# Front projections in two rounded passes, centred key weights turned on the array, and ten of sixteen heads on VectorE

## The chip, the cores and the metric

The kernel runs on one NeuronCore of a Trainium2 chip. The metric is the device time of one execution in microseconds (us); lower is better. A program is written for each engine by hand (TensorE, here PE; VectorE, DVE; ScalarE, ACT; GpSimd, POOL; SyncE, SP, which issues the loads), and the engines meet only at semaphores. Each engine runs its own list in order.

## The reference

A small network with 8 x 32 tokens of width 256 and a context of 8 x 512 tokens. The change touches only the first layer's attention, and in it the projections and the norms of their heads:

```
ln_out = LN(layernorm(x)) * ln_w + ln_b                     # 256 tokens x 256
def lin(x, w, w_scale, in_scale):
    xq = fp8(bf16(clip(x / in_scale, -448, 448)))           # rounded to 4 bits of mantissa
    return (xq * in_scale) @ w.T * w_scale
qx = LN(lin(ln_out, wqx, ...))      # 16 heads of 128
k  = LN(lin(ln_out, wk, ...))       #  8 groups of 128
q  = LN(lin(ln_out, wq, ...))       # 16 heads of 128
v  = lin(ln_out, wv, ...)           #  8 groups of 128
kx, vx = split(ctx @ w_kv_x.T);  kx = LN(kx)
cat = [softmax(q k / sqrt(128)) v, softmax(qx kx / sqrt(128)) vx]
x = x + lin(cat, wproj, ...)
```

A state-space layer, a mixture of experts, attention to the masked context, an attention with rotary positions and a table-coded feed-forward layer follow. They are as they were.

## The kernel before

The front is everything ahead of the loop over the eight batches of context. It has three strands:

- **Projections.** The weights come in six chunks of 1024 columns (`VARIANT` says which of the four input scales a chunk uses: 0 and 1 are the cross queries, 2 the keys, 3 and 4 the queries, 5 the values). `project(n)` makes four banks of 128 tokens x 512 columns, each from two products in fp32 (`CT` is 2), with the rounded inputs `xs` held in the array and the chunk `wch` streamed. An fp32 product stands in the trace as two matmul instructions, so a chunk is 16 of them. The input scale is multiplied into `xs` on DVE (L1735). Chunks use two slots of `wch`; a chunk is loaded when the one two before it has been used.
- **Head norms.** ACT reads the four banks (`read_chunk`, L1612) into one of two slots of `raw`. DVE takes the statistics of 16 heads (`norm_heads`, L1756) and prepares the variance (L1759 to L1763), ACT does Ln and Exp (L283, L284), DVE a Newton step and the shift (L263 to L1770), and then each engine scales 8 heads: DVE at L1775, ACT at L1632 in `normalise`. PE turns the 16 heads (`turn`, L1514), ACT reads them (`read_turn`, L1639).
- **Cross queries.** DVE multiplies the turned heads by a column (`read_turn_cross`, L1786); PE then makes `beta` and eight products `A` for chunk n against the centred key weights `wkc` (`cross_queries`, L1524 and L1529), each into a bank of a ring of four (`RING`) that ACT must have read (L1598, L1621) before it comes round again.

The key weights are centred twice: `wkc` (natural order) by a product with a centring matrix (L1571), and `wkT` (turned) on DVE by a sum, a scaling and a subtraction (L1743 to L1745) from a load of its own. `wk_hi` and `wk_lo` (L1659, L1800) are a rounded fp32r copy of `wkT` and what it leaves, and are needed for `keys` (L429 to L431), the first work of the loop, which already runs in rounded passes; so is `ctx_lo` (L684).

The orders are written out by hand. On PE: centre, project 0, project 1, turn 0, project 2, cross queries 0, turn 1, project 3, cross queries 1, turn 2, project 4, turn 3, project 5, core scores, then keys and turn 4. The orders on ACT and DVE are seen in the diff and in the functions below.

Of the kernel before, what the change touches and what calls it, by code (L numbers as in the profile page):

```python
# [17 lines left out]
T = B * S  # L18
# [29 lines left out]
for _name, _w in [("ident", 128), ("ones", 128), ("center", 128), ("mixed", S), ("cos", S), ("sin", S), ("iota", LUTN)]:  # L48
# [12 lines left out]
    ("ctx_hi0", CT * NK, FRONT, LOOP), ("beta", NH * T, FRONT, LAST), ("A_hi", CT * NK, FRONT, LAST),  # L61
# [5 lines left out]
    ("kT", G * T, FRONT, FRONT), ("v", TT * 1024, FRONT, FRONT), ("attn", 4 * 512, FRONT, FRONT),  # L67
# [33 lines left out]
RING = [("lnT", 4, "dve"), ("center", 4, "act")]  # L101
# [18 lines left out]
def build(nc, io, out):  # L120
    ctx = ExitStack()
    with ctx:
# [12 lines left out]
        for name in ("wkc", "wkT", "ctx_hi0", "ctx_hi1", "ctxT_ring", "A_hi", "A", "catx", "A_first", "beta"):  # L135
            tensors[name, fp32r] = tensor(name, fp32r)
# [71 lines left out]
        ld_const, ld_x, ld_wkn, ld_wkT, ld_wvT = (sem(n) for n in ("ld_const", "ld_x", "ld_wkn", "ld_wkT", "ld_wvT"))  # L208
# [13 lines left out]
        xs_ready, wk_centered, bk_ready = sem("xs_ready"), sem("wk_centered"), sem("bk_ready")  # L222
# [76 lines left out]
        def round_fp8(step, n, dst):  # L299
# [6 lines left out]
            return nc.vector.tensor_tensor(dst, dst, m_bf[:, 0:n], ALU.subtract)  # L306
# [37 lines left out]
        wpx_lo, wpx_hi = buf("A_first", NH, C, dtype=fp32r), buf("beta", NH, C, dtype=fp32r)  # L344
# [1081 lines left out]
        def _(sp):  # L1426
# [5 lines left out]
            sp.dma_start(wkT, io["wkT"]).then_inc(ld_wkT, 16)  # L1432
# [38 lines left out]
        def _(pe):  # L1471
# [19 lines left out]
            def project(n):  # L1491

                pe.wait_ge(xs_ready, SCALED.index(VARIANT[n]) + 1)
                pe.wait_ge(ld_chunk[n % 2], 16 * (n // 2 + 1))
                for q in range(4):
                    j, hf = q // 2, q % 2
                    if n:
                        pe.wait_ge(proj_read, 4 * n - 3 + q)
                    for c in range(CT):
                        last = nc.tensor.matmul(bank(q), xs[:, VARIANT[n], c, j * 128:j * 128 + 128],  # L1500
                                                wch[n % 2][:, c, hf * 512:hf * 512 + 512],
                                                start=c == 0, stop=c == CT - 1)
                    last.then_inc(proj_full, 1)

            def turn(n):
# [3 lines left out]
                for i in range(4):  # L1509
                    o = bank(ring(f"turn{n}", i), 2, T)  # L1510
                    for k in range(4):
# [3 lines left out]
                                                   raw[RAW_SLOT[n]][:, j, c0:c0 + 128], ident)  # L1515
                    last.then_inc(ring_full, 1)
# [56 lines left out]
            project(0)  # L1573
            project(1)
# [15 lines left out]
        def _(act):  # L1590
# [4 lines left out]
            def read_ring(name, i, dst, **kw):  # L1595
# [3 lines left out]
                                     ACT.Copy, **kw).then_inc(ring_read["act"], 1)  # L1599

# [24 lines left out]
            def normalise(n):  # L1625
# [4 lines left out]
                for i in range(8):  # L1630
# [12 lines left out]
            act_rstd(act, step, TT, 1)  # L1643
            for i in range(4):
# [12 lines left out]
            act.wait_ge(ring_full, RING_AT["A1"] + 8)  # L1657
            act.wait_ge(wk_centered, 1)
# [44 lines left out]
        def _(dve):  # L1703
# [21 lines left out]
            def scaled_input(n):  # L1725
# [7 lines left out]
                step(round_fp8(step, CT * T, xs[:, n].rearrange("p c t -> p (c t)")))  # L1733
                for c in range(CT):
                    last = nc.vector.tensor_scalar(xs[:, n, c, :], xs[:, n, c, :], col("in_scale", n * CT + c), None,  # L1735
                                                   ALU.mult)
                last.then_inc(xs_ready, 1)
                dve.wait_ge(xs_ready, SCALED.index(n) + 1)

            scaled_input(0)  # L1740
            dve.wait_ge(ld_wkT, 16)
            heads = wkT.rearrange("p c (g d) -> p (c g) d", g=G)
            step(nc.vector.tensor_reduce(nt[:, 0:CT * G], heads, AX, ALU.add))  # L1743
            step(nc.vector.tensor_scalar(nt[:, 0:CT * G], nt[:, 0:CT * G], 1.0 / D, None, ALU.mult))
            nc.vector.tensor_tensor(heads, heads, nt[:, 0:CT * G].unsqueeze(2).broadcast_to([128, CT * G, D]),  # L1745
                                    ALU.subtract).then_inc(wk_centered, 1)

            def norm_heads(n):
# [24 lines left out]
                for i in range(8):  # L1773
                    hd = r[:, 0, i * D:(i + 1) * D]
# [159 lines left out]
```

## Time and profile before

| | |
|---|---|
| time, median of 3 runs | 479.61 us (478.98 to 480.41) |
| the profiled execution | 483.38 us, of it the span 481.6 us |
| PE busy | 450.2 us (93%) |
| DVE busy | 352.0 us (73%) |
| ACT busy | 248.7 us (52%) |
| mean granted TensorE clock | 0.982 of full speed |

The span runs from the first to the last instruction of the profile. Busy times count an engine's instructions at work, not its waits. Lines (L1500) are those of the kernel before.

### The profile page before, as it was taken

Reading aid. Unit: us, or ns where it says so; the run is one execution under the profiler, and the core shown is the slowest. Engines: PE = TensorE matmul, PEld = TensorE weight load, DVE = VectorE, ACT = ScalarE, POOL = GpSimd, SP = SyncE. Lnnn points to the kernel's source line nnn. Section 1 sums busy time; section 2 is a strip of 40 time slices with the busy share of each in tenths; the row PEclk is TensorE's granted clock in tenths of the full one; section 3 lists DMA queues with packets and bytes.
Section 4 is the critical chain, followed back from the end, with each engine's and each line's share of the span. In section 5 each row is a group of like instructions: output and inputs, shape, how many; then the busy total and the mean of one; then the engine's idle time right before and its main releaser. Section 6 shows DMA issues by size and latency. Waiting matters only on the chain.

```text
span 481.6 us, 6644 instructions
## 1 busy us (share of the span) xinstructions
PE 450.2 (93%) x2336; PEld 304.9 (63%) x2342; DVE 352.0 (73%) x729; ACT 248.7 (52%) x784; POOL 25.5 (5%) x33
## 2 busy tenths in 40 slices
PE   5987999989999999999999999998888999989897
PEld 2442445667887676767576776856655888536566
DVE  5888495849799869698899989766776468644731
ACT  1465688997553677758986676553020205110120
POOL 0000000000110000101001010100000111100000
PEclk9999799999999999999999999999998999989999
DMA  8167020224201114693448464880068579720000
GB/s 314 82 228 297 0 88 0 79 99 160 82 0 45 44 45 109 136 319 70 110 109 172 111 131 110 177 333 0 1 206 329 176 206 222 166 85 1 1 1 22
DMA packets 14046, 58.57 MB, mean 122 GB/s; under 512 B 1792, under 2 KB 2496, under 8 KB 12480
## 3 DMA queue, kind: packets, MB, share of 16 engines
q1 hardware_dynamic: 10992, 41.66, 23.6%
q0 software_dynamic: 3024, 16.52, 17.6%
q8 instruction: 17, 0.28, 0.2%
q14 instruction: 13, 0.11, 0.1%
HBM read 41.40 MB, written 0.26 MB: 87 GB/s over the span
## 4 chain that ended last, share of the span: by engine, by line
PE 74%; DVE 12%; ACT 10%; issue 2%; DMA 1%; SPq 0%; DVEq 0%; ACTq 0%
PE PS L456 11%; PE PS L429 9%; PE PS L431 8%; PE PS L430 8%; PE PS L1043 6%; PE PS L1529 3%; PE PS L1500 3%; PE PS L476 3%; PE PS L1054 3%; ACT raw_dt.float L1632 3%; PE PS L503 2%; PE PS L1154 2%; ACT raw_dt.float L1612 2%; PE PS L465 1%; PE PS L364 1%
## 5 line engine op out<-in xcount | busy, mean ns | idle before, releaser
L576 ACT ACTIVATE sq_dt.float<-PS 128x128 bf16<-128x128 f32 x256 | 67.3, 281 | 28.9 <-PE PS L431 22.2
L456 PE MATMUL PS<-s_dt.float,ctx_ring_dt.float 128*128 128x512 f32 x128 | 57.7, 593 | 1.3 <-DVE px_dt.float L810 1.3
L429 PE MATMUL PS<-wkc_dt.float32r,ctx_hi_dt.float32r 128*128 128x512 f32 x128 | 53.7, 420 | 1.6 <-ACT sq_dt.float L576 1.2
L576 ACT ACTIVATION_READ_ACCUMULATOR sq_dt.float<-PS 128x1 f32 x256 | 53.8, 211 | 0.0
L431 PE MATMUL PS<-wkc_dt.float32r,ctxT_ring_dt.float32r 128*128 128x512 f32 x128 | 50.4, 393 | 0.0
L430 PE MATMUL PS<-wkT_dt.float32r,ctx_hi_dt.float32r 128*128 128x512 f32 x128 | 50.1, 392 | 0.0
L653 ACT ACTIVATE luttmp_dt.float<-low_bit_dt.float,vec_dt.float,small_dt.float 128x1536 f32<-128x1536 uint8 x24 | 38.5, 1656 | 10.5 <-DMA lutw_dt.float<-luttmp_dt.float 10.5
L1500 PE MATMUL PS<-wch_dt.float,xs_dt.float 128*128 128x512 f32 x96 | 42.2, 594 | 0.7 <-DVE xs_dt.float L1735 0.7
L456 PEld LDWEIGHTS PS<-s_dt.float,ctx_ring_dt.float 128*128 128x128 f32 x128 | 23.6, 190 | 25.0 <-issue 23.0
L660 DVE SCALAR_TENSOR_TENSOR luttmp_dt.float<-idx_dt.float,luttmp_dt.float 128x1536 f32<-128x1536 uint8 x21 | 36.5, 1750 | 0.0
L364 PE MATMUL PS<-consts_dt.float 128*128 128x512 bf16 x116 | 28.9, 404 | 6.0 <-DMA consts_dt.float<-in_consts 5.5
L429 PEld LDWEIGHTS PS<-wkc_dt.float32r,ctx_hi_dt.float32r 128*128 128x128 f32 x128 | 24.0, 187 | 14.1 <-ACT sq_dt.float L576 9.3
L1500 PEld LDWEIGHTS PS<-wch_dt.float,xs_dt.float 128*128 128x128 f32 x96 | 17.8, 190 | 22.3 <-issue 20.3
L666 POOL DMA_DIRECT2D lutw_dt.float<-luttmp_dt.float x21 | 18.3, 871 | 188.2 <-DVE luttmp_dt.float L660 188.2
L431 PEld LDWEIGHTS PS<-wkc_dt.float32r,ctxT_ring_dt.float32r 128*128 128x128 f32 x128 | 24.0, 188 | 5.7
L430 PEld LDWEIGHTS PS<-wkT_dt.float32r,ctx_hi_dt.float32r 128*128 128x128 f32 x128 | 24.1, 188 | 3.6
L797 DVE TENSOR_TENSOR s_dt.float<-s_dt.float,PS 128x2048 f32<-128x2048 f32 x8 | 18.3, 2288 | 10.3 <-PE PS L446 10.3
L364 PEld LDWEIGHTS PS<-consts_dt.float 128*128 128x128 bf16 x122 | 12.1, 103 | 21.0 <-DMA consts_dt.float<-in_consts 5.5
L429 PE MATMUL PS<-A_hi_dt.float32r,ctx_hi_dt.float32r 128*128 128x512 f32 x64 | 25.3, 396 | 0.0
L430 PE MATMUL PS<-A_dt.float32r,ctx_hi_dt.float32r 128*128 128x512 f32 (+1 forms) x64 | 24.9, 390 | 0.0
L431 PE MATMUL PS<-A_hi_dt.float32r,ctxT_ring_dt.float32r 128*128 128x512 f32 x64 | 24.9, 389 | 0.0
L283 ACT ACTIVATE small_dt.float<-small_dt.float 128x2 f32<-128x2 f32 (+1 forms) x12 | 3.7, 304 | 37.6 <-DVE small_dt.float L274 30.1
(272 smaller groups left out, 845.0 us busy)
## 6 DMA issues: line engine op xcount, KB each, us to landing
lutw_dt.float<-luttmp_dt.float POOLq DMA_DIRECT2D x21, 768.0 KB, 6.6
wch_dt.float<-in_chunks SPq DMA_DIRECT2D x6, 1024.0 KB, 5.0
ctxT_ring_dt.float<-in_ctxT SPq DMA_DIRECT2D x8, 512.0 KB, 4.0
ctx_ring_dt.float<-in_ctx SPq DMA_DIRECT2D x8, 512.0 KB, 3.3
keysT_dt.float<-in_ctxT SPq DMA_DIRECT2D x8, 512.0 KB, 7.6
keys_dt.float<-in_ctx SPq DMA_DIRECT2D x8, 512.0 KB, 9.3
luttmp_dt.float<-in_idx SPq DMA_DIRECT2D x3, 768.0 KB, 5.6
zu_dt.float<-in_wproj SPq DMA_DIRECT2D x1, 2048.0 KB, 7.3
```

The source lines that it names most:

```text
L364: nc.tensor.matmul(bank(nb), busy[:, 0:128], busy, start=True, stop=True)
L429: nc.tensor.matmul(o, x_hi, hi[:, c, :], start=c == 0, stop=False)
L430: nc.tensor.matmul(o, x_hi, lo[:, c, :], start=False, stop=False)
L431: last = nc.tensor.matmul(o, x_lo, hi[:, c, :], start=False, stop=c == CT - 1)
L456: last = nc.tensor.matmul(bank(5 + c), keysr[k][:, t, c * 128:c * 128 + 128], sS[k][:, t, :], start=t == 0, stop=t == KT - 1)
L576: last = nc.scalar.activation(sq[:, (4 * hf + g) * D:(4 * hf + g + 1) * D], bank(hf)[:, g * D:(g + 1) * D], ACT.Square, accum_out=ssq[:, k ...
L653: nc.scalar.activation(lutt[:, m, :], low_bit[:, m, :], ACT.Identity, scale=lut_gap[:, k:k + 1], bias=col("lut", 2 * k)).then_inc(lut_leaf, 1)
L660: nc.vector.scalar_tensor_tensor(lutt[:, m, :] if k else lutw[:, m, :], idx[:, m, :], float(2 * k), lutt[:, m, :], ALU.is_equal, ALU.mult) ...
L666: pool.dma_start(lutw[:, m, :], lutt[:, m, :], accum_op=ALU.add).then_inc(lut_added[m], 16)
L797: nc.vector.tensor_tensor(sS[k], sS[k], bank(4).unsqueeze(1).broadcast_to([128, KT, 512]), ALU.subtract)\
L1043: last = nc.tensor.matmul(o[:, m, :], wgu[e % 4][:, i, w0:w0 + 128], hT[:, c, :], start=c == 0, stop=c == CT - 1)
L1500: last = nc.tensor.matmul(bank(q), xs[:, VARIANT[n], c, j * 128:j * 128 + 128], wch[n % 2][:, c, hf * 512:hf * 512 + 512], start=c == 0, s ...
```

## The change

1. A chunk of weights is multiplied by its input scale and rounded to fp32r by ACT (`wch_hi`), DVE makes what the rounding leaves (`wch_lo`, in place of the chunk), and `project` runs an fp32r pass for each. `xs` is written in fp32r and no longer scaled (L1735 goes).
2. `wkT` is no longer loaded and centred on DVE. PE turns `wkc` (`turn_wk`, 16 transposes in four banks, between project 0 and project 1) and ACT copies it out.
3. DVE scales 10 of the 16 heads, ACT the other 6.
4. In the order of ACT `normalise(2)` moves from ahead of `read_chunk(3)` to behind `cross_queries(1)`; in that of DVE `read_turn_cross(1)` moves ahead of `norm_heads(2)`. The splits are put between.
5. Buffers: `wch_hi0`, `wch_hi1` and a `wpx_hi` of its own; `beta` gets smaller.

```diff
-RING = [("lnT", 4, "dve"), ("center", 4, "act")]
+RING = [("lnT", 4, "dve"), ("center", 4, "act"), ("wkturn", 4, "act")]
...
-            sp.dma_start(wkT, io["wkT"]).then_inc(ld_wkT, 16)
...
             def project(n):
                 pe.wait_ge(xs_ready, SCALED.index(VARIANT[n]) + 1)
-                pe.wait_ge(ld_chunk[n % 2], 16 * (n // 2 + 1))
+                pe.wait_ge(chunk_hi, n + 1)
+                pe.wait_ge(chunk_split, n + 1)
...
                     for c in range(CT):
-                        last = nc.tensor.matmul(bank(q), xs[:, VARIANT[n], c, j * 128:j * 128 + 128],
-                                                wch[n % 2][:, c, hf * 512:hf * 512 + 512],
-                                                start=c == 0, stop=c == CT - 1)
+                        xq = xs[:, VARIANT[n], c, j * 128:j * 128 + 128]
+                        nc.tensor.matmul(bank(q), xq, wch_hi[n % 2][:, c, hf * 512:hf * 512 + 512],
+                                         start=c == 0, stop=False)
+                        last = nc.tensor.matmul(bank(q), xq, wch_lo[n % 2][:, c, hf * 512:hf * 512 + 512],
+                                                start=False, stop=c == CT - 1)
...
+            def turn_wk():
+                pe.wait_ge(ring_read["act"], reads("act", RING_AT["center"] + 4))
+                for i in range(4):
+                    o, c = bank(ring("wkturn", i), 4, D), i // 2
+                    for k in range(4):
+                        last = nc.tensor.transpose(o[:, k, :], wkc[:, 4 * (i % 2) + k, c * 128:c * 128 + 128], ident)
+                    last.then_inc(ring_full, 1)
...
             project(0)
+            turn_wk()
             project(1)
...
+            def split_chunk(n):                      # ACT
+                act.wait_ge(ld_chunk[n % 2], 16 * (n // 2 + 1))
+                if n > 1:
+                    act.wait_ge(proj_full, 4 * (n - 1))
+                for c in range(CT):
+                    last = nc.scalar.activation(wch_hi[n % 2][:, c, :], wch[n % 2][:, c, :], ACT.Copy,
+                                                scale=col("in_scale", VARIANT[n] * CT + c))
+                last.then_inc(chunk_hi, 1)
...
-                for i in range(8):                   # ACT, normalise
+                for i in range(2, 8):
...
+            split_chunk(0)                           # ACT order
             for i in range(4):
                 read_ring("center", i, wkc[:, 2 * i:2 * i + 2, :])
+            split_chunk(1)
             read_chunk(0)
+            for i in range(4):
+                read_ring("wkturn", i, wkT[:, i // 2, 512 * (i % 2):512 * (i % 2) + 512])
             normalise(0)
             read_chunk(1)
+            split_chunk(2)
             read_turn(0, zlnT, "qxln_w", "qxln_b")
             normalise(1)
+            split_chunk(3)
             read_chunk(2)
             cross_queries(0)
             read_turn(1, zlnT, "qxln_w", "qxln_b")
-            normalise(2)
+            split_chunk(4)
             read_chunk(3)
             cross_queries(1)
+            normalise(2)
+            split_chunk(5)
             act.wait_ge(ring_full, RING_AT["A1"] + 8)
...
+            def split_chunk(n):                      # DVE
+                dve.wait_ge(chunk_hi, n + 1)
                 for c in range(CT):
+                    last = nc.vector.scalar_tensor_tensor(wch_lo[n % 2][:, c, :], wch[n % 2][:, c, :],
+                                                          col("in_scale", VARIANT[n] * CT + c), wch_hi[n % 2][:, c, :],
+                                                          ALU.mult, ALU.subtract)
+                last.then_inc(chunk_split, 1)
...
             scaled_input(0)
-            dve.wait_ge(ld_wkT, 16)
-            heads = wkT.rearrange("p c (g d) -> p (c g) d", g=G)
-            step(nc.vector.tensor_reduce(nt[:, 0:CT * G], heads, AX, ALU.add))
-            step(nc.vector.tensor_scalar(nt[:, 0:CT * G], nt[:, 0:CT * G], 1.0 / D, None, ALU.mult))
-            nc.vector.tensor_tensor(heads, heads, nt[:, 0:CT * G].unsqueeze(2).broadcast_to([128, CT * G, D]),
-                                    ALU.subtract).then_inc(wk_centered, 1)
+            split_chunk(0)
+            split_chunk(1)
...
-                for i in range(8):                   # DVE, norm_heads
-                    hd = r[:, 0, i * D:(i + 1) * D]
+                for i in range(10):
+                    hd = r[:, i // 8, (i % 8) * D:(i % 8 + 1) * D]
...
             norm_heads(0)                            # DVE order
             scaled_input(1)
+            split_chunk(2)
             read_turn_cross(0)
             norm_heads(1)
             scaled_input(3)
+            split_chunk(3)
+            read_turn_cross(1)
             norm_heads(2)
-            read_turn_cross(1)
+            split_chunk(4)
             scaled_input(2)
             norm_heads(3)
+            split_chunk(5)
             dve.wait_ge(wk_hi_ready, 1)
```

## Rows read from the trace of the kernel before

**Rows 1.** Page, busy time of each engine over the span

```profile
PE 450.2 (93%) x2336; PEld 304.9 (63%) x2342; DVE 352.0 (73%) x729; ACT 248.7 (52%) x784; POOL 25.5 (5%) x33
```

**Rows 2.** Windows: length, busy PE, PEld, DVE, ACT, POOL, clock, DMA share, GB/s

```profile
0.00:96.00 96.00, 83.60 (x321) 40.20 (x322) 69.98 (x249) 61.31 (x120) 0.30 (x5) 0.96 0.36 135
...
145.00:308.00 163.00, 162.63 (x680) 113.61 (x679) 142.69 (x195) 113.16 (x420) 13.36 (x17) 1.00 0.49 119
```

**Rows 3.** Chain of waits, 0 to 100 us: start, length, what

```profile
16.32 7.13 PE PS L1500 x16
...
48.31 0.49 ACT beta_dt.float L1598
...
48.84 7.45 PE PS L1529 x10
56.28 1.75 PE PS L1514 x16
58.03 6.87 PE PS L1500 x16
64.90 1.00 PE PS L1524 x8
65.90 7.08 PE PS L1529 x16
...
94.25 1.15 ACT v_dt.float L1612 x2
```

**Rows 4.** Timeline, PE: start, length, line, tile, count, idle before

```profile
16.30 14.00 PE L1500 MATMUL PS<-wch_dt.float,xs_dt.float 128*128 128x512 f32 x32
...
93.08 0.40 PE L431 MATMUL PS<-wkc_dt.float32r,ctxT_ring_dt.float32r 128*128 128x512 f32 x1
...
93.31 0.40 PE L429 MATMUL PS<-wkc_dt.float32r,ctx_hi_dt.float32r 128*128 128x512 f32 x1
```

**Rows 5.** Timeline, DVE

```profile
15.63 0.62 DVE L1735 TENSOR_SCALAR xs_dt.float<-xs_dt.float,vec_dt.float 128x256 f32<-128x256 f32 x2
...
18.82 2.29 DVE L1745 TENSOR_TENSOR wkT_dt.float<-wkT_dt.float,small_dt.float 128x2048 f32<-128x2048 f32 x1
...
28.45 2.14 DVE L1775 TENSOR_SCALAR raw_dt.float<-raw_dt.float,small_dt.float 128x128 f32<-128x128 f32 x8
...
37.03 3.18 DVE L1756 BATCH_NORM_STATS2 small_dt.float<-raw_dt.float 128x6 f32<-128x128 f32 x16
...
60.13 0.17 DVE L263 TENSOR_TENSOR small_dt.float<-small_dt.float 128x16 f32<-128x16 f32 x1 [6.91 <-ACT small_dt.float L284]
...
63.15 1.68 DVE L1786 TENSOR_SCALAR zu_dt.float<-zu_dt.float,vec_dt.float 128x512 f32<-128x512 f32 x4
...
141.79 1.22 DVE L680 TENSOR_TENSOR A_dt.float32r<-A_dt.float,A_hi_dt.float32r 128x1024 fp32r<-128x1024 f32 x1
142.92 1.22 DVE L684 TENSOR_TENSOR ctxT_ring_dt.float32r<-ctxT_ring_dt.float,ctx_hi_dt.float32r 128x1024 fp32r<-128x1024 f32 x1
...
157.35 1.75 DVE L660 SCALAR_TENSOR_TENSOR lutw_dt.float<-idx_dt.float,luttmp_dt.float 128x1536 f32<-128x1536 uint8 x1
```

**Rows 6.** Timeline, ACT

```profile
16.36 0.60 ACT L1598 ACTIVATE wkc_dt.float<-PS 128x512 f32<-128x512 f32 x1 [0.26 <-PE PS L1571]
...
31.55 2.38 ACT L1612 ACTIVATE raw_dt.float<-PS,vec_dt.float 128x512 f32<-128x512 f32 x4
...
42.82 3.19 ACT L1632 ACTIVATE raw_dt.float<-raw_dt.float,small_dt.float 128x128 f32<-128x128 f32 x8 [0.93 <-DVE small_dt.float L1770]
...
59.47 0.32 ACT L283 ACTIVATE small_dt.float<-small_dt.float 128x16 f32<-128x16 f32 x1
...
60.97 3.19 ACT L1632 ACTIVATE raw_dt.float<-raw_dt.float,small_dt.float 128x128 f32<-128x128 f32 x8 [0.93 <-DVE small_dt.float L1770]
...
82.53 1.04 ACT L1663 ACTIVATE ctx_hi_dt.float32r<-ctxT_ring_dt.float 128x1024 fp32r<-128x1024 f32 x1
```

**Rows 7.** Timeline, PE, the three turns that end a front stage

```profile
31.74 1.94 PE L1514 MATMUL PS<-consts_dt.float,raw_dt.float 128*128 128x128 f32 x16 [1.44 <-issue]
...
72.80 1.91 PE L1514 MATMUL PS<-consts_dt.float,raw_dt.float 128*128 128x128 f32 x16
...
82.73 1.94 PE L1514 MATMUL PS<-consts_dt.float,raw_dt.float 128*128 128x128 f32 x16 [1.15 <-issue]
```

**Rows 8.** Windows (columns as in rows 2) around 50 us and behind the front

```profile
45.30:48.80 3.50, 0.00 (x0) 0.00 (x0) 3.26 (x10) 3.50 (x8) 0.00 (x0) 0.87 0.13 54
...
52.00:54.00 2.00, 2.00 (x3) 0.67 (x2) 1.05 (x6) 0.60 (x1) 0.00 (x0) 0.50 0.00 0
...
97.00:102.00 5.00, 3.58 (x25) 2.55 (x25) 2.95 (x5) 5.00 (x22) 0.00 (x0) 1.00 0.40 170
```

More of the change, by code:

```diff
@@ L60 @@
     ("wkT", CT * G * D, FRONT, LOOP), ("wvT", CT * G * D, FRONT, LAST), ("wkc", G * C, FRONT, LOOP),
-    ("ctx_hi0", CT * NK, FRONT, LOOP), ("beta", NH * T, FRONT, LAST), ("A_hi", CT * NK, FRONT, LAST),
+    ("ctx_hi0", CT * NK, FRONT, LOOP), ("beta", 4 * T, FRONT, LOOP), ("wch_hi0", 3072, FRONT, LOOP),
+    ("wpx_hi", NH * C, LAST, LAST, "beta"), ("A_hi", CT * NK, FRONT, LAST),
     ("sq", 512, FRONT, LAST), ("qfront", 1024, FRONT, LAST),
@@ L134, in build @@
         tensors = {(name, fp32): tensor(name, fp32) for name in size}
-        for name in ("wkc", "wkT", "ctx_hi0", "ctx_hi1", "ctxT_ring", "A_hi", "A", "catx", "A_first", "beta"):
+        for name in ("wkc", "wkT", "ctx_hi0", "ctx_hi1", "ctxT_ring", "A_hi", "A", "catx", "A_first", "wpx_hi", "xs", "wch",
+                     "wch_hi0", "wch_hi1"):
             tensors[name, fp32r] = tensor(name, fp32r)
@@ L205, in build @@
         h, hT = buf("h", TT, C), buf("hT", CT, T)
-        ld_const, ld_x, ld_wkn, ld_wkT, ld_wvT = (sem(n) for n in ("ld_const", "ld_x", "ld_wkn", "ld_wkT", "ld_wvT"))
+        ld_const, ld_x, ld_wkn, ld_wvT = (sem(n) for n in ("ld_const", "ld_x", "ld_wkn", "ld_wvT"))
         ld_chunk = [sem("ld_chunk0"), sem("ld_chunk1")]
@@ L297, in build, with round_fp8 @@
         t_q = buf("qtmp", 512, skip=768)
-        def round_fp8(step, n, dst):
+        def round_fp8(step, n, dst, out=None):
             step(nc.vector.tensor_scalar(m_bf[:, 0:n].bitcast(u16), y_bf[:, 0:n].bitcast(u16), 0x7F80, None,
@@ L305, in round_fp8 @@
             step(nc.vector.tensor_tensor(dst, y_bf[:, 0:n], m_bf[:, 0:n], ALU.add))
-            return nc.vector.tensor_tensor(dst, dst, m_bf[:, 0:n], ALU.subtract)
+            return nc.vector.tensor_tensor(dst if out is None else out, dst, m_bf[:, 0:n], ALU.subtract)
         wkn = buf("raw", G * C, skip=2048)
@@ L313, in build @@
         wpc = buf("zu", NH, C)
+        wch_hi = [buf(f"wch_hi{k}", CT, 1024, dtype=fp32r) for k in range(2)]
+        wch_lo = [buf("wch", CT, 1024, skip=2048 * k, dtype=fp32r) for k in range(2)]
         raw = [buf("raw", TT, 1024), buf("raw", TT, 1024, skip=2048)]
         RAW_SLOT = {0: 0, 1: 1, 2: 0, 3: 1, 4: 0}
-        lnT, xs = buf("lnT", CT, T), buf("xs", 4, CT, T)
+        lnT, xs = buf("lnT", CT, T), buf("xs", 4, CT, T, dtype=fp32r)
+        xs_wide = buf("xs", 4 * CT * T)
         zlnT, uT, kT, v = buf("zu", 8, T), buf("zu", 8, T, skip=8 * T), buf("kT", G, T), buf("v", TT, 1024)
@@ L343, in build @@
         wpx = buf("A_first", NH, C)
-        wpx_lo, wpx_hi = buf("A_first", NH, C, dtype=fp32r), buf("beta", NH, C, dtype=fp32r)
+        wpx_lo, wpx_hi = buf("A_first", NH, C, dtype=fp32r), buf("wpx_hi", NH, C, dtype=fp32r)
         betaT = buf("qfront", 4, T)
@@ L1653, in _ @@
             read_turn(1, zlnT, "qxln_w", "qxln_b")
-            normalise(2)
+            split_chunk(4)
             read_chunk(3)
             cross_queries(1)
+            normalise(2)
+            split_chunk(5)
             act.wait_ge(ring_full, RING_AT["A1"] + 8)
-            act.wait_ge(wk_centered, 1)
+            act.wait_ge(ring_read["act"], reads("act", RING_AT["wkturn"] + 4))
             nc.scalar.activation(wk_hi, wkT, ACT.Copy).then_inc(wk_hi_ready, 1)
@@ L1912 @@
         "chunks": np.stack([tiles(w.T) for w in chunks]),
-        "wkT": tiles(wkv[:1024].T), "wvT": tiles(wkv[1024:].T), "wproj": tiles(a[X + "wproj"].T),
+        "wvT": tiles(wkv[1024:].T), "wproj": tiles(a[X + "wproj"].T),
         "ctxT": ctx.reshape(B, NK, CT, 128).transpose(0, 3, 2, 1), "ctx": ctx.reshape(B, KT, 128, C).transpose(0, 2, 1, 3),
```

14 lines of the change are left out of this document (7 added, 7 removed).

## The prediction, on record before the change was run

> **What bounds the kernel now.** I read the page's busy times first: PE is at work for 450.2 of 481.6 us [rows 1]. That is an average. The windows then split it: from 145 to 308 us, the loop, PE is busy for 162.6 of 163 us, but in the 96 us of the front, the only place that the change touches, PE has 83.6, DVE 70.0 and ACT 61.3 [rows 2]. So in the loop PE is the bound and a late start shifts it whole; in the front the reader must ask which wait ends last. The chain of waits answers: in the first 96 us it passes through only two projections on PE, chunk 0 (7.13 us at 16.3) and chunk 3 (6.87 us at 58.0); at the other places it goes DVE statistics, ACT Ln and Exp, DVE Newton, ACT heads, ACT reads [rows 3]. PE's projections of chunks 1, 2, 4 and 5 lie beside that.
>
> **Prices.** Projection: 32 fp32 instructions take 14.0 us, 0.44 each, so 7.0 us a chunk; the loop's fp32r passes of the same width start 0.23 us apart (93.08, 93.31), so 16 take 3.7 us [rows 4]. PE saves 3.3 a chunk, 20 us in all.
> ACT's rounding (hi): two of 128x1024. L1663 of that shape takes 1.04 [rows 6], a pair 2.0 with the overlap of neighbours that four neighbouring L1612 reads show (2.38 for four of 0.69, so 0.57 apart [rows 6]). Its scale is a column, as L1612's is; bounds 1.9 to 2.3.
> DVE's rest (lo): two of 128x1024 with two fp32 sources; neighbours L680 and L684 start 1.13 apart and last 1.22 [rows 5], so 2.35. The operation (scalar_tensor_tensor in fp32r) is not shown in this shape; L660 is one, 1.75 for 1536 elements [rows 5], 1.17 per 1024. Bounds 2.0 to 2.8.
> Heads: DVE 2.14 for eight, so 2.7 for ten [rows 5]; ACT 3.19 for eight, so 2.4 for six [rows 6].
> Statistics 3.2 [rows 5], from their end (40.2) to the scaling (42.8) 2.6 when ACT is free [rows 5, 6]; 1.5 of it from ACT's Ln (59.47) to the scaling (60.97) [rows 6], 1.1 before. Reading a chunk 2.3. Column products of the turned heads 1.7 [rows 5]. The scaled input without L1735 takes 3.1 instead of 3.7 (0.62 goes [rows 5]).
>
> The Trainium skill (ScalarE: Activation LUTs, What ACT_TABLE_LOAD costs) has a column operand add 93 ns to an ACTIVATE even back to back. Rows 6 show it in the length (0.69 against 0.60) but not in the distance of neighbours (0.57). By the page each hi would take about 0.17 more, three lie on the path below, and the sum would be 0.5 higher.
>
> **The path, stage by stage, new against before.**
>
> A. The input is ready at 15.6 instead of 16.3. But lo of chunk 0 follows it on the same engine: 15.6 + 2.35 = 18.0. The hi before it is hidden under DVE's layer norm. Project 0 runs 18.0 to 21.7 (before to 23.4 [rows 3]). Chunk 1: ACT's last centre read ends at 17.0 [rows 6], hi to 19.0, lo to 21.3; only then the statistics of chunk 0, which wait behind it: to 24.5, + 2.6 = 27.1. Before, heads were scaled at 28.45 [rows 5]: 1.4 gained of 1.7. Turn 0 at 27.1 + 2.7 = 29.8, before 31.7 [rows 7]. The removed centring of `wkT` (L1745 alone 2.29 [rows 5]) lay in DVE's wait for chunk 0 and gives nothing itself; the turning of `wkc` on PE (16 transposes, 1.8) and ACT's four reads (22.3 to 24.7) end before ACT is wanted at 25.6. If that cover went, they would cost 2.3. One load less moves chunk 1 earlier, which nobody waits for; SP is passed by nothing else.
>
> B. ACT has scaled its six heads at 29.5, reads chunk 1 to 31.8, and now stands 2.0 in hi 2, to 33.8, where before it read turn 0 at once. DVE waits for that: lo 2 ends at 36.2, the column products behind it at 37.9 (before 37.0, where the statistics start [rows 5]), statistics 41.1, scaling 43.7 (before 42.8 [rows 6]): 0.9 lost. ACT's six heads end at 46.1, hi 3 at 48.1, the read of chunk 2 at 50.4, beta at 50.9; before 48.8 [rows 3]. **2.1 late.** PE has done three A products by 43.5 and waits 7.4 us, before 3.5 [rows 8].
>
> C. From here PE is the chain, as before: the rest of A 7.45 and turn 1 1.75 [rows 3], to 60.1; project 3 in 3.7, to 63.8; beta 1.0 and A 7.1 [rows 3], to 71.9. Before 73.0. **1.1 early**: chunk 3 is the one place where the faster pass pays whole.
>
> D. Before, turn 2 followed at once at 72.8 [rows 7], for its heads had been scaled from 60.97 on [rows 6], under project 3. Now `normalise(2)` stands behind the last A read (72.5): + 1.5 = 74.0, ten heads to 76.7. DVE has been blocked in `norm_heads(2)` since about 64, and lo 4, the input for chunk 5 and the statistics of chunk 3 are queued behind that wait; before, DVE waited 6.9 us in the same place [rows 5] but had all of it done by 73. Now: lo 4 79.1, input 82.2, statistics 85.4, + 2.6 = 88.0, ten heads 90.7. Turn 3 at 90.7, before 82.7 [rows 7]. **8.0 late**: turn 2 is 3.9 late, and from it to turn 3 it now takes 14.0 us of DVE in a row where it took 9.9 of ACT's work.
>
> E. Behind it on DVE: lo 5 93.1, wk_lo (2.29, as L1745) 95.3, ctx_lo 1.1 96.4, statistics of chunk 4 99.6, + 2.6 = 102.2, ACT's six heads 104.6. Before, that point was 94.25 [rows 3]. **10.3 late.**
>
> Behind it the chain is ACT's (second half of the values, A_hi, squares, exp, reads), unchanged. Project 4 and 5 run in 3.7 each and no one feels it. Buffers cost nothing: no transfer gets a new wait on the path (a chunk lands well ahead of its hi).
>
> The sum: 481.6 + 10.3 = 491.9 of span, 493.7 with what lies around it (483.4 now). The profiled execution is 3.8 above the median; I add the difference to the median: 479.6 + 10.3 = **490 us** (about 2.1% slower). Bounds: hi at 1.9 and lo at 2.0 (five lo on the path) give 8.2, hi at 2.3 and lo at 2.8 give 13.5.
>
> **Rivals.**
>
> 1. TensorE's passes are the bound (faster). PE is 87% busy in the front (83.6 of 96 [rows 2]), and if the splits lay wholly beside it and the scaling of chunk 2 still ended under project 3, the two projections on the chain would give 2 x 3.3 = 6.6, less about 0.6 kept at chunk 0: 474. Against it: PE waits 3.5 us for ACT at 45.3 already [rows 8], and the DVE stalls in D come from written order. It decides only if turn 2 is ready by 72.
> 2. The half clock. In the window 52 to 54 us PE ran at 0.50 of the granted clock, 1.2 GHz, after 3.5 idle us, and ten instructions that need 4.3 took 7.45 [rows 3, 8]: 3.1 lost. The new front has gaps of 7.4 (B), 4.8 (D), about 8 (ahead of turn 3) and 4 (ahead of turn 4). Those of D and of turn 3 fall where DVE is the chain; if those behind turn 3 and 4 are felt, one or two times 2 to 3 come on top: 494. The Trainium skill (TensorE: Matmul & The Clock Gate, What's actually happening) says likewise that idleness takes the array to the lower of two clocks; by it every one of these gaps would do so.
> 3. Part is caught up. Between 97 and 102 us PE idles 1.4 [rows 8]; the first keys, done ahead of a late turn 4, might give as much again: 10.3 less about 3 gives 487.
> 4. Gains and losses cancel, 479 to 481: only if DVE could take lo 4 and the input inside the wait of D, which the order forbids, or if the splits cost half.
>
> **Chances.** My sum 0.48, rival 2 0.18, rival 3 0.20, rival 1 0.09, rival 4 0.05. Range: from rival 3 with the low split prices (484.5) to rival 2 (495); that leaves out rivals 1 and 4 and about 6% at the ends. A measurement can tell 0.3% (1.4 us) from no change: slower 0.86, same 0.05, faster 0.09.
>
> **What would show it.** Projections in about 3.7 us; their first pass at 18.0, right behind a pair of DVE operations of 2.35; a PE gap near 7 us that ends with ACT's read of beta near 51; cross queries 1 ended near 72, and then turn 2 not before 76; DVE idle for over 6 us in front of L263 of chunk 2; turn 3 near 91 and the loop's rows shifted by 10 us, their lengths unchanged. I am wrong if turn 2 follows the last A product at once, if DVE gets past `norm_heads(2)` before ACT's last A read, or if the pair of splits takes far less than 4 us.

## The result, and the profile after

The changed kernel takes 491.38 us (median of 4, 488.08 to 492.62) against 480.01 us (median of 4) for the kernel before: ratio 1.0232, 95% interval 1.0182 to 1.0281, so about 11 us slower. The forecast was 490 us. All ratios here compare the fast executions of each kernel, and the profiled execution of the kernel before is a slow one: 483.38 us at a mean granted clock of 0.982, where others went down to 474.91 us at 1.0.

The page's first section for the changed kernel, to be held against [rows 1]:

```profile
PE 439.1 (90%) x2358; PEld 312.8 (64%) x2358; DVE 361.3 (74%) x740; ACT 259.1 (53%) x790; POOL 25.5 (5%) x33
```

TensorE works 11.1 us less, and the program is longer. Where the time went shows in the windows (columns as in [rows 2]):

```profile
0.00:96.00 96.00, 66.66 (x248) 42.93 (x249) 70.09 (x221) 66.27 (x114) 0.30 (x5) 0.86 0.31 116
...
155.00:318.00 163.00, 162.63 (x679) 113.63 (x678) 142.72 (x195) 113.15 (x420) 13.35 (x17) 1.00 0.49 118
```

The second line is the 145 to 308 us window of before, 10 us later, and its sums are equal to a few hundredths. In the first 96 us TensorE is busy 66.7 us where it was 83.6: it has more to wait for, not less to do at the end.

A marker dates this in every trace: VectorE's first addition of 128x2048 in the loop. The line is from the timeline of VectorE, before at 130.32, here:

```profile
140.49 2.29 DVE L803 TENSOR_TENSOR s_dt.float<-s_dt.float,PS 128x2048 f32<-128x2048 f32 x1 [2.62 <-PE PS L452]
170.61 2.29 DVE L803 TENSOR_TENSOR s_dt.float<-s_dt.float,PS 128x2048 f32<-128x2048 f32 x1 [1.34 <-PE PS L452]
```

The next one follows in 30.12 us, as before (160.44). So **the loop starts 10.17 us late** in these two executions, and that is the change. The two profiled spans differ by only 7.3 us (488.9 and 481.6) for another reason, seen in two windows that cover the same work at the end, of before and then of after:

```profile
364.12:481.60 117.48, 106.62 (x705) 78.58 (x708) 63.01 (x146) 22.04 (x38) 7.34 (x8) 0.96 0.42 114
```

```profile
374.30:488.90 114.60, 104.87 (x710) 77.25 (x708) 62.60 (x146) 21.92 (x38) 7.34 (x8) 0.97 0.42 116
```

That untouched tail took 2.9 us more in the profiled execution of before. Spans of single executions are therefore off by up to 3 us either way for reasons outside the front. The marker is free of that, but not of what differs inside the front from one execution to the next; where that shows, the text says so.

The timeline of VectorE in the changed kernel, the lines of the forecast's stages B to E:

```profile
33.47 2.48 DVE L1776 SCALAR_TENSOR_TENSOR wch_dt.float32r<-wch_dt.float,vec_dt.float,wch_hi_dt.float32r 128x1024 fp32r<-128x1024 f32 x2 [1.16 <-ACT wch_hi_dt.float32r L1624]
...
72.79 0.17 DVE L266 TENSOR_TENSOR small_dt.float<-small_dt.float 128x16 f32<-128x16 f32 x1 [6.40 <-ACT small_dt.float L287]
...
73.63 2.65 DVE L1811 TENSOR_SCALAR raw_dt.float<-raw_dt.float,small_dt.float 128x128 f32<-128x128 f32 x10
76.31 2.48 DVE L1776 SCALAR_TENSOR_TENSOR wch_dt.float32r<-wch_dt.float,vec_dt.float,wch_hi_dt.float32r 128x1024 fp32r<-128x1024 f32 x2
...
81.80 3.19 DVE L1792 BATCH_NORM_STATS2 small_dt.float<-raw_dt.float 128x6 f32<-128x128 f32 x16
...
87.58 2.65 DVE L1811 TENSOR_SCALAR raw_dt.float<-raw_dt.float,small_dt.float 128x128 f32<-128x128 f32 x10
90.27 2.48 DVE L1776 SCALAR_TENSOR_TENSOR wch_dt.float32r<-wch_dt.float,vec_dt.float,wch_hi_dt.float32r 128x1024 fp32r<-128x1024 f32 x2
92.67 2.29 DVE L1840 TENSOR_TENSOR wkT_dt.float32r<-wkT_dt.float,wkc_dt.float32r 128x2048 fp32r<-128x2048 f32 x1
```

Read it from 72.79: VectorE has stood idle 6.40 us in front of one small operation, with the split, the input and the statistics of the next chunk queued behind; then it works from 73.6 to 100.4 with one hole of 0.47 us (at 86.3, in front of the same small operation), and TensorE's turns wait for it. ScalarE's rounding holds up its own reads in the same way (stage B of the forecast). TensorE's timeline shows both sides, the projection's passes 0.23 apart and the turns that wait:

```profile
60.20 0.39 PE L1507 MATMUL PS<-wch_hi_dt.float32r,xs_dt.float32r 128*128 128x512 f32 x1
60.43 0.40 PE L1509 MATMUL PS<-wch_dt.float32r,xs_dt.float32r 128*128 128x512 f32 x1
...
64.49 7.13 PE L1546 MATMUL PS<-zu_dt.float,wkc_dt.float 128*128 128x512 f32 x16
76.33 3.68 PE L1522 MATMUL PS<-consts_dt.float,raw_dt.float 128*128 128x128 f32 x16 [4.71 <-DVE raw_dt.float L1811]
...
90.29 3.68 PE L1522 MATMUL PS<-consts_dt.float,raw_dt.float 128*128 128x128 f32 x16 [6.29 <-DVE raw_dt.float L1811]
```

Against [rows 7], turn 2 starts 3.5 us later (72.80) and turn 3 7.6 us later (82.73). Each turn also lasts twice as long as before (3.68, not 1.91): the granted clock was 0.50 in 76.3 to 80.0 us and in 90.3 to 93.6 us.

### The profile page after: what moved, and what is told of

It is laid out like the page before. It is cut to its first block, busy times and chain, and to the rows that moved or that the text cites. A ratio compares the mean times of both kernels' runs of the same rounds, so it can differ in the third digit from the quotient of the medians.

```text
span 488.9 us, 6710 instructions
## 1 busy us (share of the span) xinstructions
PE 439.1 (90%) x2358; PEld 312.8 (64%) x2358; DVE 361.3 (74%) x740; ACT 259.1 (53%) x790; POOL 25.5 (5%) x33
## 4 chain that ended last, share of the span: by engine, by line
PE 69%; DVE 18%; ACT 9%; issue 2%; DMA 2%; SPq 0%; DVEq 0%; ACTq 0%
PE PS L462 11%; PE PS L435 9%; PE PS L437 8%; PE PS L436 8%; PE PS L1049 6%; PE PS L1546 3%; DVE small_dt.float L1792 3%; PE PS L1060 2%; PE PS L509 2%; PE PS L1160 2%; PE PS L482 2%; DVE wch_dt.float32r L1776 2%; ACT sq_dt.float L582 2%; PE PS L471 1%; ACT raw_dt.float L1659 1%
## 5 line engine op out<-in xcount | busy, mean ns | idle before, releaser
L1522 PE MATMUL PS<-consts_dt.float,raw_dt.float 128*128 128x128 f32 x80 | 16.5, 391 | 16.1 <-DVE raw_dt.float L1811 16.1
L1522 PEld LDWEIGHTS PS<-consts_dt.float,raw_dt.float 128*128 128x128 f32 x80 | 14.8, 208 | 18.8 <-DVE raw_dt.float L1811 18.2
L286 ACT ACTIVATE small_dt.float<-small_dt.float 128x2 f32<-128x2 f32 (+1 forms) x12 | 3.6, 300 | 43.5 <-DVE small_dt.float L277 30.1
L1507 PE MATMUL PS<-wch_hi_dt.float32r,xs_dt.float32r 128*128 128x512 f32 x48 | 20.8, 434 | 5.3 <-DVE wch_dt.float32r L1776 5.3
```

Of the source, the lines that this page charges most:

```text
L1507: nc.tensor.matmul(bank(q), xq, wch_hi[n % 2][:, c, hf * 512:hf * 512 + 512], start=c == 0, stop=False)
L1522: last = nc.tensor.transpose(o[:, hd, j * 128:j * 128 + 128], raw[RAW_SLOT[n]][:, j, c0:c0 + 128], ident)
```

## The experiments

All ratios are to the kernel before, timed beside each experiment. A marker is one execution. All markers are in one table at the end of the section, with the time from the start of turn 1 to the marker beside them: the splits of chunks 0 to 3 and the first A products lie ahead of turn 1; chunk 3's passes, the moved order and the splits of chunks 4 and 5 lie behind it.

**1. The order put back.** On both engines the one move of the order is undone, the rest of the change stays:

```diff
-            split_chunk(4)
-            read_chunk(3)
-            cross_queries(1)
             normalise(2)
+            split_chunk(4)
+            read_chunk(3)
+            cross_queries(1)
...
-            read_turn_cross(1)
             norm_heads(2)
+            read_turn_cross(1)
```

> The changed kernel with the one move of the order undone: normalise(2) again ahead of read_chunk(3) on ScalarE, norm_heads(2) again ahead of read_turn_cross(1) on VectorE; splits, ten heads and turned weights stay. My theory (the order costs the wait ahead of turn 2): the TensorE gap ahead of turn 2 goes from 4.7 us to under 1, the last product of A ends 2 to 3 us later than in the changed kernel, ScalarE's six heads of chunk 4 end about 4.5 us earlier (near 99.7 instead of 104.2), time about 487 (1.014 of before). Rival (TensorE's passes or the half clock set the end): the same time as the changed kernel, 491.

Median 489.0 us, ratio 1.0254 (1.0200 to 1.0309); marker 135.32, **5.2 us earlier** than in the changed kernel. The time does not show it: the ratio is no lower than the changed kernel's 1.0232, though 5.2 us would be 0.011. What the order does is read from the trace. TensorE's timeline:

```profile
50.93 6.06 PE L1546 MATMUL PS<-zu_dt.float,wkc_dt.float 128*128 128x512 f32 x10 [5.08 <-ACT beta_dt.float L1616]
...
66.09 7.47 PE L1546 MATMUL PS<-zu_dt.float,wkc_dt.float 128*128 128x512 f32 x16 [2.68 <-DVE zu_dt.float L1822]
73.40 1.91 PE L1522 MATMUL PS<-consts_dt.float,raw_dt.float 128*128 128x128 f32 x16
```

The wait has moved from turn 2 to the second A (2.68 us), where it costs less, and turn 2 follows at once. Not all of the 5.2 is the order's: the first line shows the first A products, ahead of anything that was moved. In the changed kernel they stand so:

```profile
50.56 7.60 PE L1546 MATMUL PS<-zu_dt.float,wkc_dt.float 128*128 128x512 f32 x10 [5.08 <-ACT beta_dt.float L1616]
```

After the same wait of 5.08 us the half clock lasted 1.5 us less in experiment 1's execution. From the start of turn 1 to the marker, where only the order differs, it is 78.5 us against 82.5: the order costs **4.0 us** there.

**2. One pass in place of two.** TensorE's lo pass is left out, both splits are still made:

```diff
-                        nc.tensor.matmul(bank(q), xq, wch_hi[...], start=c == 0, stop=False)
-                        last = nc.tensor.matmul(bank(q), xq, wch_lo[...], start=False, stop=c == CT - 1)
+                        last = nc.tensor.matmul(bank(q), xq, wch_hi[...], start=c == 0, stop=c == CT - 1)
```

> The changed kernel with the second (lo) pass of every projection left out on TensorE, both splits still made: the projections use the rounded weights alone. 48 passes fewer, 11 us of TensorE. My theory (only chunk 3's passes are on the chain): 1.5 to 1.9 us less than the changed kernel, 489.5. Rival (TensorE's passes bound the front): all 11 us come back, or at least the passes of chunks 0, 3 and 4, 5 to 11 us: 480 to 486.

Median 486.33, ratio 1.0199 (1.0141 to 1.0257); marker 138.45, 2.0 earlier for 11 us less of TensorE. Project 3 ends 1.8 us sooner after turn 1 at half its passes, but the A products behind it then wait 0.88 us for ScalarE, and turn 2 comes only 0.7 us nearer to turn 1. Another 0.8 of the 2.0 lies ahead of turn 1, where the ten products at the half clock took 6.15 us in this execution and not 7.60. The median is 5 us below the changed kernel's, but the kernel before was also faster beside it; the ratios, 1.0199 and 1.0232, are 1.6 us apart and their intervals overlap.

**3. VectorE's split left out.** The second pass runs on hi again:

```diff
-                        last = nc.tensor.matmul(bank(q), xq, wch_lo[n % 2][...],
+                        last = nc.tensor.matmul(bank(q), xq, wch_hi[n % 2][...],
...
-            split_chunk(0) ... split_chunk(5)        # VectorE's six calls
```

> The changed kernel with VectorE's lo split left out; TensorE's second pass runs on the hi part once more, so the output leaves out what the rounding of the weights leaves and counts the rest twice; TensorE's and ScalarE's work stay. My theory: lo of chunks 1, 2, 4 and 5 are on the path at 2.4 us each, so 8.5 to 9.7 us less than the changed kernel: 482 (1.005 of before). Rival (ScalarE's hi is the late one and VectorE only waits for it): under 3 us less, 489.

Median 483.63, ratio 1.0120 (1.0065 to 1.0175); marker 134.35, 6.1 earlier, less than the 8.5 to 9.7 I gave. The heads show where:

```profile
25.59 2.65 DVE L1808 TENSOR_SCALAR raw_dt.float<-raw_dt.float,small_dt.float 128x128 f32<-128x128 f32 x10
...
41.27 2.65 DVE L1808 TENSOR_SCALAR raw_dt.float<-raw_dt.float,small_dt.float 128x128 f32<-128x128 f32 x10
...
70.89 2.65 DVE L1808 TENSOR_SCALAR raw_dt.float<-raw_dt.float,small_dt.float 128x128 f32<-128x128 f32 x10
...
82.45 2.65 DVE L1808 TENSOR_SCALAR raw_dt.float<-raw_dt.float,small_dt.float 128x128 f32<-128x128 f32 x10
...
94.28 2.65 DVE L1808 TENSOR_SCALAR raw_dt.float<-raw_dt.float,small_dt.float 128x128 f32<-128x128 f32 x10
```

Against 26.57, 43.24, 73.63, 87.58 and 101.80 in the changed kernel the gain is 1.0, 2.0, 2.7, 5.1 and 7.5. The splits of chunks 4 and 5 give their full 2.4; those of chunks 0, 1 and 2 together give 2.0, because the reads of chunk 0 (the statistics start at 19.54, after a wait for them) and ScalarE's own work then end the waits. The next 0.8 is again a shorter stretch at the half clock (the ten products of A took 6.82 us and not 7.60), so the split of chunk 3 gives nothing. Between the last heads and the marker 1.4 is lost.

**4. Only the ten heads,** on the kernel before:

```diff
-                for i in range(8):           # ScalarE
+                for i in range(2, 8):
...
-                for i in range(8):           # VectorE
-                    hd = r[:, 0, i * D:(i + 1) * D]
+                for i in range(10):
+                    hd = r[:, i // 8, (i % 8) * D:(i % 8 + 1) * D]
```

> The kernel before with only the ten and six heads of the change. My theory: ScalarE is the later engine of each scaling by 1.05 us, so the scaling of chunks 0, 1, 3 and 4 gets 0.4 to 0.8 us shorter and the TensorE gap at 45 us falls below 3.5 us, which may spare the half-clock stretch (3 us): 1 to 4 us less than before, 476 to 479. Rival (the heads are beside the chain): 480.

Median 477.72 (10 runs), ratio 0.9963 (0.9924 to 1.0002); marker 125.67, 4.65 earlier than before. The wait ahead of the last A products and what follows it:

```profile
46.96 4.56 PE L1529 MATMUL PS<-zu_dt.float,wkc_dt.float 128*128 128x512 f32 x10 [1.70 <-ACT beta_dt.float L1598]
```

It was 3.5 us [rows 8] and the ten instructions took 7.45 [rows 3]. Of the 4.65, 2.9 are the half clock that did not come. By the marker the heads are the good part of the change; the time does not show a gain, since the interval reaches 1.0, and some executions of the kernel before lack the half clock too (a mean granted clock of 1.0 leaves no room for it).

**5 and 6. Back to fp32 projections,** with the moved order, and with the order undone too:

```diff
-                pe.wait_ge(chunk_hi, n + 1)
-                pe.wait_ge(chunk_split, n + 1)
+                pe.wait_ge(ld_chunk[n % 2], 16 * (n // 2 + 1))
...          (one fp32 product of wch, xs scaled on VectorE as before, no split_chunk on either engine)
```

> The changed kernel with its first part undone: fp32 projections, scaled inputs, no splits on ScalarE and VectorE; turned key weights, ten heads and the moved order stay. Marker: the start of VectorE's first 128x2048 addition of the loop (130.3 us in the kernel before, 140.5 in the changed one, 125.7 with only the ten heads). My theory: the splits are the larger share of the loss, the marker falls by about 7 to 133.5, the moved order stays in it (a TensorE gap of 4 us or more ahead of turn 2); time 482. Rival (the order is the larger share): the marker stays at 136 or more.

Median 484.56, ratio 1.0125 (1.0062 to 1.0188); marker 134.49, 6.0 earlier than the changed kernel.

> As the run with fp32 projections, and the move of normalise(2) and read_turn_cross(1) undone too: the kernel before with the ten heads and the turned key weights. My theory: the turned weights cost nothing (1.8 us of TensorE and 2.3 of ScalarE beside the chain, 4.8 of VectorE taken out of a wait): the marker is 126 to 127, as with the ten heads alone, time 477. Rival (the 16 transposes lie between project 0 and project 1 and delay the reads that normalise(0) queues behind): 128 or more.

Median 477.77 (10 runs), ratio 0.9980 (0.9946 to 1.0013); marker 126.53. TensorE's timeline of experiment 5 shows what the order alone does where nothing is split:

```profile
61.73 7.13 PE L1543 MATMUL PS<-zu_dt.float,wkc_dt.float 128*128 128x512 f32 x16
73.57 3.67 PE L1519 MATMUL PS<-consts_dt.float,raw_dt.float 128*128 128x128 f32 x16 [4.71 <-DVE raw_dt.float L1803]
77.04 8.11 PE L1506 MATMUL PS<-wch_dt.float,xs_dt.float 128*128 128x512 f32 x16
```

The same 4.71 us of wait as in the changed kernel. With fp32 projections the move costs 134.49 - 126.53 = **8.0 us**, 7.5 of it behind turn 1, and here the times agree: 1.0125 against 0.9980 is 7.0 us. With split projections it was 4.0 behind turn 1. The splits show their cost ahead of turn 1: it starts at 52.02 here and at 58.00 in the changed kernel, 2.9 from the later start of the ten A products, though the changed kernel's front was 0.8 us ahead, and 3.0 from their half clock (7.60 us, not 4.56). Behind turn 1 the two kernels take the same time, 82.5 us: chunk 3's faster passes, 3.2 us by the end of A, give back about what the splits of chunks 4 and 5 cost.

**7. Filling the long wait** in the changed kernel:

```diff
             project(2)
+            keep_clock(20, ring("A0"))
             cross_queries(0)
```

> The changed kernel with 20 matmuls of 128x512 bf16 (nothing reads them) on TensorE between project 2 and cross queries 0, 4.3 us of filling in a wait of 7. My theory for this stretch: the half clock after the wait lengthens the ten products of A from 4.3 to 7.6 us, and they are on the chain; with the filling they take 4.5 and the marker falls by 3, to 137.5. Rival (the half clock is beside the chain, or comes anyway): marker at 140.5.

Median 487.68, ratio 1.0219 (1.0139 to 1.0298); marker 137.08, 3.4 earlier; the time, 1.0219 against 1.0232, does not resolve that. The last ten instructions of A take 4.56 us in place of 7.60, though 20 matmuls were added, and turn 1 starts 2.6 us earlier in an execution whose front ran 0.45 late from the start; the remaining 0.8 comes behind turn 1, with no cause that I can name. The half clocks at turn 2, 3 and 4 (3.67, 3.68, 3.56) are still there.

**8. Splitting the inputs instead of the weights.** The weights come from fp8 and stream as loaded; the scaled input of 256x256 is what needs two parts. VectorE makes both from the rounded input, on the kernel before with the ten heads (the main lines; the chunks' loads on SP go, and those on GpSimd write an fp32r buffer):

```diff
-                    last = nc.vector.tensor_scalar(xs[:, n, c, :], xs[:, n, c, :], col("in_scale", ...), None, ALU.mult)
+                    last = nc.vector.tensor_scalar(xs_hi[:, n, c, :], xs[:, n, c, :], col("in_scale", ...), None, ALU.mult)
+                step(last)
+                for c in range(CT):
+                    last = nc.vector.scalar_tensor_tensor(xs_lo[:, n, c, :], xs[:, n, c, :], col("in_scale", ...),
+                                                          xs_hi[:, n, c, :], ALU.mult, ALU.subtract)
...
+            for n in range(NCH):             # GpSimd, in place of SP
+                if n > 1:
+                    pool.wait_ge(proj_full, 4 * (n - 1))
+                pool.dma_start(wch_r[n % 2], io["chunks"][n]).then_inc(ld_chunk[n % 2], 16)
```

> A version that should beat both: the kernel before with the ten heads, and two fp32r passes made by splitting the inputs (256x256 for each of four scales) in place of the chunks: VectorE makes hi as the scaled input and lo as the rest, the weights stream as loaded. ScalarE has no split; VectorE has two more operations of 128x256 for each scale, 0.8 us. The chunks are loaded from GpSimd's queue. If the path is what I say (splits of chunks on it, passes mostly beside it), the marker is 124 to 128 and the time 474 to 478. Rival (the fp32r passes themselves or GpSimd's loads cost something the rows do not show): 480 or more.

A miss: median 482.49 (10 runs), ratio 1.0073 (1.0038 to 1.0108), marker 132.46. The cause is in its first line on TensorE:

```profile
10.26 5.57 PE L366 MATMUL PS<-consts_dt.float 128*128 128x512 bf16 x14 [10.26 <-DMA consts_dt.float<-in_consts]
```

The constants landed at 10.3 us, 5.46 in the kernel before. GpSimd had its two loads of 1 MB issued by 2.6 us. And the centring of `wkT` on VectorE, which in the kernel before fills a wait, now stood on the chain (22.0 to 26.8). Of the 6.8 us by which the marker is later than experiment 4's, 4.6 are there at turn 0, and 1.7 are a half clock on the ten products of A (6.26 us, not 4.56).

**9. Both mended:** experiment 6's kernel with the inputs split, and GpSimd's first load behind the constants:

```diff
+            pool.wait_ge(ld_const, 32)
             for n in range(NCH):
```

> The inputs split again, on the fp32 version with ten heads, turned key weights and the order of before (marker 126.5), and GpSimd's chunk loads held back until the constants have landed. Two faults of the first such run go with it: the constants landed at 10.2 us instead of 5.4 because GpSimd's two loads were on the wire before them, and the centring on VectorE (4.8 us) stood between the inputs and the first statistics. My theory: heads of chunk 0 scaled at 26 us (28.2 in the fp32 version), a wait of 4 to 5 us ahead of the last products of the first A with the half clock behind it (3 us), marker 124 to 128. Rival (the passes give more than that): 122 or less. Time 474 to 479.

Median 476.23 (12 runs), ratio 0.9939 (0.9898 to 0.9979). The marker, 128.78, is above my 124 to 128. The profiled execution took 480.89 us, with the lowest mean granted clock of the twelve (0.964), and the half clock shows in both stretches of A:

```profile
45.75 6.25 PE L1541 MATMUL PS<-zu_dt.float,wkc_dt.float 128*128 128x512 f32 x10 [3.36 <-ACT beta_dt.float L1611]
...
61.11 10.16 PE L1541 MATMUL PS<-zu_dt.float,wkc_dt.float 128*128 128x512 f32 x16 [2.70 <-DVE zu_dt.float L1821]
```

**10. The same with filling** (14 matmuls at the place of experiment 7).

> The same with 14 matmuls of filling (3 us) between project 2 and cross queries 0. If the half clock behind that wait is on the chain, the marker falls by up to 3 us against the run without filling, to 123 to 125; if the wait was too short to bring it, by nothing. Time 472 to 478.

Median 476.65 (12 runs), ratio 0.9937 (0.9901 to 0.9974); marker 124.84, the earliest of all. The two A stretches take 4.56 and 8.73. The marker is 3.9 us before experiment 9's and the time is the same, so the filling is not shown to pay here.

**11. The kernel before with 8 matmuls of filling** at that place.

> The kernel before with 8 matmuls of filling (1.7 us) between project 2 and cross queries 0 and nothing else. My theory: the half-clock stretch of before (ten instructions in 7.45 us instead of 4.4) goes, the marker falls from 130.3 to 127.3. The time falls by 3 us if the runs without a profile have that stretch too, by less if they mostly do not. Rival (the stretch is set by something else than the wait): marker 130.

Median 477.64 (12 runs), ratio 0.9942 (0.9911 to 0.9973); marker 128.58. The ten instructions take 4.56; its front ran 0.9 us late from the start (heads of chunk 0 at 29.33, before 28.45), and with that taken off the marker gains 2.6. Here the time agrees: 0.58% is 2.8 us. The mean granted clock was 1.0 in five of the twelve runs; of 29 runs of the kernel before beside them, two reached 0.999 or more.

| kernel | marker, us | against the changed one | against before | turn 1 to marker |
|---|---|---|---|---|
| before | 130.32 | -10.2 | | 74.2 |
| changed | 140.49 | | +10.2 | 82.5 |
| 1 order put back | 135.32 | -5.2 | +5.0 | 78.5 |
| 2 hi pass only | 138.45 | -2.0 | +8.1 | 81.3 |
| 3 no lo on VectorE | 134.35 | -6.1 | +4.0 | 79.1 |
| 4 before, ten heads | 125.67 | | -4.7 | 74.3 |
| 5 fp32 passes, new order | 134.49 | -6.0 | +4.2 | 82.5 |
| 6 fp32 passes, old order | 126.53 | -14.0 | -3.8 | 74.9 |
| 7 changed, filled | 137.08 | -3.4 | +6.8 | 81.7 |
| 8 inputs split | 132.46 | | +2.1 | 73.9 |
| 9 the same, mended | 128.78 | | -1.5 | 76.9 |
| 10 mended and filled | 124.84 | | -5.5 | 75.1 |
| 11 before, filled | 128.58 | | -1.7 | 74.5 |

## Why the prediction was right, step by step

The four parts of the change, added one at a time (experiments 4, 6, 5, changed), give for the marker: ten heads -4.65, turned key weights +0.86, the moved order +7.96, the split projections +6.00. That these sum to the measured +10.17 proves nothing, since each is the difference to the one before. They are single executions, and kernels equal up to a point differed there by 0.4 to 0.9 us, so the 0.86 is not told from zero. Of the heads' gain 2.9 us, and of the splits' cost 3.0, are the half clock on the same ten products, taken away by one and brought back by the other. The order of adding matters too: the move is worth 8.0 in the fp32 kernel and 5.2, of which the trace gives it 4.0, in the changed one.

- **Stage A** (heads of chunk 0 at 27.1): 26.57. TensorE's first work, which nothing in the change touches, took 4.90 us in this execution and 5.58 before, and the front ran 0.7 us ahead from the centring on. Project 0 started at 17.56, forecast at 18.0.
- **Stage B** (scaling 43.7, beta read at 50.9, TensorE waiting 7.4): 43.24, 50.5, and a wait from 45.5 to 50.56, 5.1 us. The three A products ended at 45.5 and not at 43.5, because project 2 ran its first half at the half clock (passes 0.43 apart, the clock 0.66 in 36 to 41 us). Nobody felt it.
- **Stage C** (A done at 71.9): 71.6. Here the faster pass came back: from turn 1 to the end of A it is 13.6 us, and 16.8 in experiment 5 with fp32 passes.
- **Stage D** (turn 2 at 76.7, turn 3 at 90.7): 76.33 and 90.29. The mechanism, statistics and split queued behind a wait that ends with ScalarE's last A read, is shown by experiments 1, 5 and 6.
- **Stage E** (ScalarE's heads of chunk 4 from 102.2): 101.79. Their end, the last point of the sum, came at 104.1, so 9.9 us late and not 10.3. With the 0.7 that this execution was ahead it would be 10.6, so part of the close agreement is luck.
- **Terms of the sum.** VectorE's pair took 2.48, not 2.35, and ScalarE's 2.17 to 2.20, not 2.0. The second is the case where I set a row against the Trainium skill and chose wrongly. I had read 0.57 as the distance of neighbours in both reads, but the rows had no run of neighbours without a column to set beside it. In the changed kernel four copies without a column run 2.06 in all, 0.49 apart, and four with one 2.39, 0.57 apart:

```profile
22.07 2.06 ACT L1616 ACTIVATE wkT_dt.float<-PS 128x512 f32<-128x512 f32 x4
...
28.89 2.39 ACT L1639 ACTIVATE raw_dt.float<-PS,vec_dt.float 128x512 f32<-128x512 f32 x4
...
31.18 2.19 ACT L1624 ACTIVATE wch_hi_dt.float32r<-wch_dt.float,vec_dt.float 128x1024 fp32r<-128x1024 f32 x2
```

  So the column costs about 0.08 even back to back. The Trainium skill (ScalarE: Activation LUTs, What ACT_TABLE_LOAD costs) gives about 93 ns for it. An estimate from the Trainium skill's figures in that section makes the pair 2.17, and the trace agrees (2.17 to 2.20).
- **A reason that was too large.** I counted four or five splits of VectorE on the path at 2.35 each. Experiment 3 shows two at full price, 2.0 for the first three together, and nothing for chunk 3's. The total held because the other waits (ScalarE's hi, the reads) stand right beside them: taking one cause away uncovers the next.
- **A slip in the range.** Rival 3 with the low split prices is 479.6 + 8.2 - 3 = 484.8, not 484.5; it changes nothing.
- **Rival 1** (TensorE's passes are the bound) fell: halving them gave 2.0 of 11 us. **Rival 2** (half clock) is half right: 3.0 us of it are on the chain in the changed kernel, but 2.9 were there before as well. The new stretches at turns 2 and 3 lie beside VectorE's chain of stage D and E. The one at turn 4 does not show either: from its start to the marker it is 35.2 to 36.3 us in the four kernels where that turn ran at the half clock and 34.9 to 37.1 in the others. **Rival 3** (part is caught up) fell: 9.9 us late at the end of stage E, 10.17 at the marker. **Rival 4** fell with them.

Experiments 9 and 10 beat the kernel before by 0.6%, and so does experiment 11, which only adds eight matmuls that nobody reads (0.9942). The gain of the two-pass projections over the ten heads alone (0.9963) is within the intervals. Whether they gain anything beyond the heads and the filling stays open.

## What to carry to other kernels

A faster pass on the busiest engine pays only where that engine ends the wait; here it was busy 87% of the front and 11 us of its work could be removed for 2 us. Before moving an operation in a hand-written order, list what is queued behind it on the same engine: `norm_heads(2)` was blocked by one small operation for about as long as before (6.40 us, 6.91 before), but the wait ended at 72.8 us and not at 60.1, and the input and the statistics that used to run under the A products ran after them. In the fp32 kernel that one move cost more (8.0 us) than all splits did later (6.0). Here the input and the weight both come from fp8, and only the scale needs the second part, so it can go into either. Put it into the smaller operand: 256x256 for each of four scales instead of 256x1024 for each of six chunks took ScalarE's 13 us of rounding away altogether. Hold a gain in a trace against the times: here markers of single executions moved by 3 to 5 us where the ratios did not tell the kernels apart (experiments 1, 4, 7 and 10).

## What the runs showed of the hardware that was not expected

- The half clock came after shorter waits than the 3.5 us of before. In the changed kernel turn 0 followed a wait of 2.44 us and took 3.59 us at a granted clock of 0.60 and then 0.54; in the kernel before it followed 1.44 and took 1.94 [rows 7]. The windows of the changed kernel:

```profile
23.00:29.00 6.00, 3.83 (x18) 2.85 (x16) 5.17 (x25) 4.08 (x12) 0.00 (x0) 1.00 0.58 195
29.00:31.00 2.00, 1.72 (x9) 1.73 (x10) 1.83 (x7) 2.00 (x4) 0.00 (x0) 0.60 1.00 410
31.00:33.00 2.00, 1.87 (x9) 1.47 (x7) 1.28 (x2) 2.00 (x3) 0.00 (x0) 0.54 1.00 408
```

  Ahead of it TensorE had been busy 3.8 of 6 us; in the kernel before it had run its two projections without a break (14.00 us [rows 4]) up to its shorter wait. Whether the longer wait or the thinner work ahead of it brings the half clock, no run here separates.
- Equal waits were not followed by equal stretches: behind 5.08 us the same ten products took 7.60 us in one execution and 6.06 in another, and the sixteen transposes of turn 0 took 3.59 us behind 2.44, 3.30 behind 2.42 and 2.78 behind 3.65 (changed kernel, experiments 1 and 3).
- Filling that nobody reads took the half clock off the ten products (4.56 us): by the trace 3.0 us in the changed kernel (20 matmuls), which the time does not resolve, and 2.6 to 2.9 in the kernel before (8 matmuls), where the time fell by 2.8.
- Two 1 MB loads issued from GpSimd at the start put off the landing of the constants, issued from SP at 1.65 us, from 5.5 to 10.3 us. With GpSimd's first load held behind them they landed at 5.8 (experiment 9).
